# Sums by destination over a span of 64 nodes instead of 128 in a graph network kernel

## The chip, the cores and the metric

The kernel runs on one core of a Trainium2 chip. The metric is the time of one execution on the device, in microseconds (us), as the median of several runs. The engines are TensorE (PE, with its weight loads listed as PEld), VectorE (DVE), ScalarE (ACT), GpSimd (POOL) and SyncE (SP). SP issues most of the plain transfers, POOL the indirect ones.

## The reference, cut to what matters

There are 6250 nodes with 128 features and 206250 directed edges, sorted by their destination `dst`. Each node is also an edge to itself in that list. Two layers follow one another:

```python
edge_index = jnp.stack([src, dst])
h = jnp.maximum(_layernorm(x), 0.0)
# layer 0: row = src, col = dst, self loops added, deg = segment_sum(w, row)
#   w_norm = dinv[row] * w * dinv[col];  out = segment_sum(w_norm * (h @ kernel)[col], row)
x = x + relu(out + bias)
h = jnp.maximum(_layernorm(x), 0.0)
# layer 1: heads = src, tails = dst
#   msg_fwd  = concat(h[src], edge_attr) @ W_fwd  + b_fwd   -> summed at dst
#   msg_back = concat(h[dst], edge_attr) @ W_back + b_back  -> summed at src
#   divided by the number of messages, leaky relu, + h, layer norm with gamma and beta
x = x + layer1(...)
```

By linearity the kernel sums raw rows first and multiplies by the weights at the end. It so needs, among others, the sum of `edge_attr` rows by `src` and the sum of `edge_attr` rows by `dst`. The second of these is what the change is about, along with one step of layer 0.

## The kernel before, in words

The edges are cut into 202 groups of 1024 (`GE`), each as 128 partitions by 8 chunks (`J`). Since edges are sorted by `dst`, a group touches a short run of consecutive destinations. 206250 / 6250 is 33 edges for each node, so 1024 edges cover about 31 nodes. The first destination of a group is its base (`base_i`), and `rel` is `dst` minus the base. `setup_and_degrees` computes both, and sets a flag when any `rel` is above 127 or below 0; then a general path without spans is taken (`nc.Else`), else the path described here. The span ("window") of a group is the 128 nodes from its base on.

`first_layer` treats groups 0 to 107 (`G1` = 108) together with half of layer 0. `dense_sums` treats the other 94 (`NB`) together with dense products over 25 double tiles of nodes: six groups ahead of the first tile, then four with each of 22 tiles. The last three tiles have no groups beside them. Both hold the same pieces for each group, in an order written out by hand for each engine:

- SP loads `rel` of the group broadcast to all partitions (`rel_b`, first layer only), the source keys in the same way (`key_b`), the records (`rec`), the 128 rows of `g` from the base on (`window`, first layer only) and the 1024 edge attributes (`attrs`).
- DVE's `prepare`, one step a chunk, compares keys (`same`) and in the first layer, at chunk 2, builds `spread_hot` (L857): partition n, column e is 1 where edge e has `rel` = n. DVE's `spot_sums` (L828, L1690) builds `sum_hot`: for each edge on a partition and each of 8 chunks, a one-hot of its `rel`. It waits until TensorE is through with the group before.
- TensorE's `spread` (L952, first layer only) multiplies `spread_hot` by `window`, so that each edge gets the row of `g` of its destination. `sum_chunk` (L965, L1815) multiplies the chunk's attributes, as the loaded weights, with `sum_hot` as the moving operand; 8 of them add up in one PSUM bank, `win_bank`. At chunk 2 it first waits for `window_added` and `sum_ready`, and then makes the products of chunks 0, 1 and 2 at once. Each float32 product is two weight loads and two matmuls in the trace. L969, L970 and L1817 multiply by `same`, for the sums by source.
- DVE's `add_window` (L837, L1699) adds `win_bank` to `attr_sums` at the base. It stands right behind `spot_sums` in DVE's order, and both stand at chunk 0 of a group.
- ACT copies the sums by source out of PSUM (L1042, L1898), and POOL adds them to tables in DRAM with one indirect DMA for each chunk (L814, L1646), in four tables in turn.

Around them in `dense_sums`: DVE's `one_hots` (L1742, L1746, L1747) and the additions L1782; TensorE's L1797 (pair counts), L1853 and L1873 (products of counts and features), L1838 (transposes). In the first layer: DVE's L885, L886, L891 and L900, and TensorE's L1001, L979 and L991.

Of the kernel before, what the change touches and what calls it, by code (L numbers as in the profile page):

```python
# [29 lines left out]
BF16 = mybir.dt.bfloat16  # L30
I16 = mybir.dt.int16
I32 = mybir.dt.int32
ALU = mybir.AluOpType
# [5 lines left out]
F = 128  # L39
P = 128  # L40
NP, NT = 125, 50
J = 8
# [27 lines left out]
GPI = 4  # L70
G1 = GPI * (2 * DS + 1)
# [32 lines left out]
def setup_and_degrees(nc, d):  # L104
# [4 lines left out]
    with ExitStack() as ctx:  # L109
# [236 lines left out]
        def _(dve):  # L346
# [94 lines left out]
            def offsets():  # L441
# [9 lines left out]
                nc.vector.tensor_scalar(wide[:, 0:1], wide[:, 0:1], P - 0.5, None, ALU.is_gt)  # L451
# [228 lines left out]
def first_layer(nc, d):  # L680
# [10 lines left out]
    with ExitStack() as ctx:  # L691
# [14 lines left out]
        rel_b = sb("rel_b", [P, 2, P, J], BF16)  # L706
        window = sb("window", [P, 2, F])
        attrs = sb("attrs", [P, 2, J, F])
        spread_hot = sb("spread_hot", [P, J, P])
        same = sb("same", [P, J, P])  # L710
        sum_hot = sb("sum_hot", [P, J, P])
# [62 lines left out]
        def _(sp):  # L774
            everywhere = lambda a, g: a[group_at(g)].rearrange("(o e) -> o e", o=1).to_broadcast([P, GE])
            flat = lambda t: t.rearrange("p q j -> p (q j)")

            def slot(i, kk, last):
                k = 2 * i + kk
                for gi in range(GPI):  # L780
# [3 lines left out]
                    sp.dma_start(flat(rel_b[:, h, :, :]), everywhere(d.dst_offset, g)).then_inc(rel_in[h], 16)  # L784
                    sp.dma_start(flat(key_b[:, h, :, :]), everywhere(d.src_key, g)).then_inc(key_in[h], 16)
# [6 lines left out]
                    sp.dma_start(window[:, h, :], d.g[bass.ds(base, P), :]).then_inc(window_in[h], 16)  # L792
# [31 lines left out]
        def _(dve):  # L824
            def spot_sums(g, h):

                at_least(dve, summed, J * g)
                nc.vector.tensor_tensor(sum_hot[:], iota_c.unsqueeze(1).to_broadcast([P, J, P]), rec[:, h, 2, :].unsqueeze(2).to_broadcast([P, J, P]),  # L828
                                        ALU.is_equal).then_inc(sum_ready, 1)

            def add_window(g):
# [4 lines left out]
                at = bass.ds(base, P)  # L836
                nc.vector.tensor_tensor(d.attr_sums[:, at], d.attr_sums[:, at], win_bank[:, 0:P], ALU.add).then_inc(window_added, 1)  # L837

            def prepare(i, kk, gi, j, ahead):
# [103 lines left out]
        def _(pe):  # L943
# [11 lines left out]
            def sum_chunk(i, kk, gi, j):  # L955
# [8 lines left out]
                for jj in (range(3) if j == 2 else range(j, j + 1) if j > 2 else ()):  # L964
                    nc.tensor.matmul(win_bank[:, 0:P], attrs[:, h, jj, :], sum_hot[:, jj, :], start=(jj == 0), stop=(jj == J - 1))  # L965
# [490 lines left out]
def dense_sums(nc, d):  # L1456
# [10 lines left out]
    with ExitStack() as ctx:  # L1467
# [38 lines left out]
        sum_hot = shared(J * P).rearrange("p (j q) -> p j q", j=J)  # L1506
# [159 lines left out]
        def _(dve):  # L1666
# [20 lines left out]
            def spot_sums(q, p):  # L1687

                at_least(dve, chunk_done, J * q)
                nc.vector.tensor_tensor(sum_hot, d.iota[:].unsqueeze(1).to_broadcast([P, J, P]), rec[:, p, 2, :].unsqueeze(2).to_broadcast([P, J, P]),  # L1690
                                        ALU.is_equal).then_inc(sum_ready, 1)

            def add_window(q):
# [4 lines left out]
                here = bass.ds(base, P)  # L1698
# [615 lines left out]
```

## Time and profile before

| | us |
|---|---|
| median of 3 runs | 4362.68 (4362.0 to 4367.89) |
| profiled execution, its own time | 4383.92 |
| span of the profiled execution | 4382.1 |
| setup | 0 to 478 |
| first layer, 108 groups | 478 to 2206 |
| end of layer 0, node by node | 2206 to 2413 |
| dense sums, six groups ahead | 2413 to 2500 |
| dense sums, 22 tiles with four groups each | 2500 to 4066 |
| dense sums, last tiles | 4066 to 4188 |
| last nodes | 4188 to 4382 |

The profile gives for each engine the time it was busy, and for each instruction the idle time ahead of it and what ended that. "Granted clock" is the share of TensorE's full clock of 2.4 GHz that it had; 0.50 is 1.2 GHz. The stages' bounds are read from the first and last indirect DMA of each stage and the first instructions of the next.

### The profile page before, as it was taken

How to read it: one execution, taken by the hardware profiler on the slowest of the kernel's cores; microseconds unless marked ns; L12 is line 12 of the kernel's file. 1: busy time of each engine (PE TensorE's matmuls, PEld its weight loads, DVE VectorE, ACT ScalarE, POOL GpSimd, SP SyncE). 2: the span in 40 equal slices, each digit the busy share in tenths (PEclk: the TensorE clock that was granted, in tenths of full speed). 3: DMA queues.
4: the chain of work that ended last, by engine and by line, in shares of the span. 5: the costliest groups of instructions: out<-in, count | busy, mean ns of one | idle time of the engine just before them, and what ended most of it. 6: DMA issues, size and time to landing. Idle time of an engine off the chain costs nothing. (4 is left out here: it accounts for less than half of the span.)

```text
span 4382.1 us, 100155 instructions
## 1 busy us (share of the span) xinstructions
PE 3372.6 (77%) x30313; PEld 2825.5 (64%) x30529; DVE 3169.7 (72%) x8053; ACT 1866.7 (43%) x4498; POOL 3001.3 (68%) x1812
## 2 busy tenths in 40 slices
PE   1444599888888988889712599888988898889945
PEld 1344587777777877777612577676767676777635
DVE  6999898888888888888524777666666666666427
ACT  1030355555555555555404244444444444444513
POOL 2665588888888888888810788777777777788210
PEclk9989899999999999999956699999999999999977
DMA  9990678777777777877785555445444544454861
GB/s 162 290 212 14 134 143 143 138 139 142 138 139 143 135 139 142 142 138 143 116 148 122 89 85 83 76 78 82 77 76 77 79 77 78 76 83 72 97 124 30
DMA packets 682053, 504.17 MB, mean 115 GB/s; under 512 B 308854, under 2 KB 593920, under 8 KB 679754
## 3 DMA queue, kind: packets, MB, share of 16 engines
q0 software_dynamic: 260032, 176.60, 36.2%
q1 hardware_dynamic: 421475, 320.75, 29.6%
q8 instruction: 287, 4.70, 0.4%
q14 instruction: 259, 2.12, 0.2%
HBM read 283.43 MB, written 240.12 MB: 119 GB/s over the span
## 5 line engine op out<-in xcount | busy, mean ns | idle before, releaser
L1646 POOL DMA_INDIRECT gcn_sums<-shared,ds_to_i x752 | 1290.0, 1715 | 569.8 <-ACT shared L1898 353.6
L814 POOL DMA_INDIRECT gcn_sums<-fl_sums,fl_to_i x864 | 1439.0, 1665 | 290.0 <-DMA gcn_sums<-fl_sums,fl_to_i 149.1
L1853 PE MATMUL bank<-ds_counts,ds_parts 128*128 128x256 bf16 x3675 | 605.9, 278 | 0.0
L1922 ACT COPY ds_turned<-bank 128x1024 bf16<-128x1024 bf16 (+1 forms) x325 | 313.1, 963 | 619.0 <-PE bank L1838 619.0
L1042 ACT COPY fl_sums<-bank 128x256 f32<-128x256 f32 x864 | 324.8, 376 | 575.4 <-PE bank L970 504.5
L1886 ACT CAST ds_counts<-bank 128x392 bf16<-128x392 f32 x800 | 382.2, 490 | 228.9 <-PE bank L1797 216.2
L852 DVE SCALAR_TENSOR_TENSOR fl_same<-fl_key_b,fl_pat,bank 128x128 f32<-128x128 bf16 x864 | 371.6, 442 | 102.7 <-PE bank L970 85.7
L1873 PE MATMUL bank<-ds_turned,ds_now 128*128 128x512 bf16 (+1 forms) x1734 | 434.3, 382 | 11.3
L1782 DVE TENSOR_TENSOR src_sums<-src_sums,bank 128x512 f32<-128x512 f32 (+1 forms) x325 | 213.2, 656 | 292.4 <-PE bank L1873 287.8
L1815 PE MATMUL bank<-shared 128*128 128x128 f32 x1504 | 304.3, 306 | 119.3 <-DVE attr_sums L1699 91.3
L1712 DVE SCALAR_TENSOR_TENSOR shared<-shared,ds_pat,from_me 128x128 f32<-128x128 bf16 x752 | 312.7, 443 | 103.9 <-PE bank L1817 92.4
L965 PEld LDWEIGHTS bank<-fl_sum_hot,fl_attrs 128*128 128x128 f32 x1728 | 263.8, 192 | 184.3 <-issue 112.2
L969 PE MATMUL bank<-fl_pay,fl_same 128*128 128x128 f32 x1728 | 349.3, 285 | 41.6 <-issue 31.4
L1817 PE MATMUL bank<-shared 128*128 128x128 f32 x1504 | 318.4, 295 | 75.3 <-DVE shared L1712 52.3
L965 PE MATMUL bank<-fl_sum_hot,fl_attrs 128*128 128x128 f32 x1728 | 324.4, 290 | 57.5 <-DVE attr_sums L837 57.3
L1853 PEld LDWEIGHTS bank<-ds_counts,ds_parts 128*128 128x128 bf16 x3675 | 344.8, 100 | 32.2
L1001 PE MATMUL bank<-fl_hi_w,fl_lo_hot 128*128 128x98 bf16 x4992 | 288.9, 208 | 83.7 <-DVE fl_hi_w L891 83.7
L970 PE MATMUL bank<-fl_attrs,fl_same 128*128 128x128 f32 x1728 | 340.9, 280 | 0.0
L991 PE MATMUL bank<-fl_turned,fl_g_tile 128*128 128x512 f32 (+1 forms) x676 | 333.3, 575 | 3.7 <-DVE gcn_t L900 1.6
L969 PEld LDWEIGHTS bank<-fl_pay,fl_same 128*128 128x128 f32 x1728 | 273.9, 196 | 82.9 <-issue 71.0
L1001 PEld LDWEIGHTS bank<-fl_hi_w,fl_lo_hot 128*128 128x128 bf16 x4992 | 257.1, 98 | 106.8 <-issue 87.5
L891 DVE TENSOR_TENSOR fl_hi_w<-fl_hi_hot,fl_twos 128x784 bf16<-128x784 bf16 x624 | 317.2, 564 | 8.7
(256 smaller groups left out, 7004.1 us busy)
## 6 DMA issues: line engine op xcount, KB each, us to landing
fl_attrs<-in_edge_attr SPq DMA_DIRECT2D x108, 512.0 KB
shared<-in_edge_attr SPq DMA_DIRECT2D x186, 256.0 KB
fl_rel_b<-dst_offset SPq DMA_DIRECT2D x108, 256.0 KB
fl_key_b<-src_key SPq DMA_DIRECT2D x108, 256.0 KB
gcn_sums<-zeros SPq DMA_DIRECT2D x40, 640.0 KB
shared<-src_key SPq DMA_DIRECT2D x94, 256.0 KB
gcn_sums<-fl_sums,fl_to_i POOLq DMA_INDIRECT x864
near<-src_float SPq DMA_DIRECT2D x1, 12892.0 KB
```

Source lines behind the costliest of these rows:

```text
L814: nc.gpsimd.indirect_dma_start(out=d.tab_gcn[j % K], out_offset=bass.IndirectOffsetOnAxis(ap=to_i[:, (GPI * kk + gi) % 4, j:j + 1], axis=0 ...
L852: nc.vector.scalar_tensor_tensor(same[:, j, :], key_p[:, h, :, j], pat_f[:, j:j + 1], from_me_c, ALU.is_equal, ALU.mult, accum_out=later[: ...
L965: nc.tensor.matmul(win_bank[:, 0:P], attrs[:, h, jj, :], sum_hot[:, jj, :], start=(jj == 0), stop=(jj == J - 1))
L969: nc.tensor.matmul(sum_bank[j % 2][:, 0:F], same[:, j, :], pay[:, j // U, j % U, :], start=True, stop=True)
L970: nc.tensor.matmul(sum_bank[j % 2][:, F:2 * F], same[:, j, :], attrs[:, h, j, :], start=True, stop=True).then_inc(summed, 1)
L991: nc.tensor.matmul(prod_bank[:, 0:n], g_tile[:, old, :], turned[:, (old + b) % 2, 0:n], start=True, stop=True).then_inc(prod_ready, 1)
L1001: last = nc.tensor.matmul(pair_bank[:, c * HH:(c + 1) * HH], lo_hot[:, go % 2, q, :], hi_w[:, go % 2, m, q, :], start=(m == 0), stop=(m == 2))
L1042: nc.scalar.copy(sums[:, h, j, :], sum_bank[j % 2][:, 0:2 * F]).then_inc(staged, 1)
L1646: nc.gpsimd.indirect_dma_start(out=d.tab_gcn[j % K].rearrange("n (two f) -> (n two) f", two=2), out_offset=bass.IndirectOffsetOnAxis(ap=to ...
L1853: ins = nc.tensor.matmul(row_bank[:, 0:2 * P], parts[:, tile, s, :], counts[:, h, tile, :, :].rearrange("p b q -> p (b q)"), start=(tile = ...
L1873: ins = nc.tensor.matmul(back_bank[v][:, 0:n], now[:, h, half, s, :], turned[:, v, half, 0:n], start=(half == 0 and s == 0), stop=(half == ...
L1886: nc.scalar.copy(to, pair_bank[batch % B][:, 0:PB * HH].rearrange("p (c k) -> p k c", c=PB)).then_inc(pair_copied, 1)
```

## The change

A constant `W` = 64 takes the place of 128 as the width of the span. In both passes `sum_hot` is built for 64 columns instead of 128, the products with it have 64 moving columns, and `add_window` adds 64. In the first layer `rel_b`, `window` and `spread_hot` have 64 partitions: the two transfers are half as large, the compare L857 runs on half the partitions with the same number of columns, and the product `spread` sums over 64 rows. The flag for the general path is set from `rel` above 63. The number of instructions, of transfers and of waits, and their order, stay.

```diff
+W = 64
...
-                nc.vector.tensor_scalar(wide[:, 0:1], wide[:, 0:1], P - 0.5, None, ALU.is_gt)
+                nc.vector.tensor_scalar(wide[:, 0:1], wide[:, 0:1], W - 0.5, None, ALU.is_gt)
...
-        rel_b = sb("rel_b", [P, 2, P, J], BF16)
-        window = sb("window", [P, 2, F])
+        rel_b = sb("rel_b", [W, 2, P, J], BF16)
+        window = sb("window", [W, 2, F])
...
-        spread_hot = sb("spread_hot", [P, J, P])
+        spread_hot = sb("spread_hot", [W, J, P])
...
-        sum_hot = sb("sum_hot", [P, J, P])
+        sum_hot = sb("sum_hot", [P, J, W])
...
-                    sp.dma_start(flat(rel_b[:, h, :, :]), everywhere(d.dst_offset, g)).then_inc(rel_in[h], 16)
+                    sp.dma_start(flat(rel_b[:, h, :, :]), everywhere(d.dst_offset, g, W)).then_inc(rel_in[h], 16)
...
-                    sp.dma_start(window[:, h, :], d.g[bass.ds(base, P), :]).then_inc(window_in[h], 16)
+                    sp.dma_start(window[:, h, :], d.g[bass.ds(base, W), :]).then_inc(window_in[h], 16)
...
-                nc.vector.tensor_tensor(sum_hot[:], iota_c.unsqueeze(1).to_broadcast([P, J, P]), rec[:, h, 2, :].unsqueeze(2).to_broadcast([P, J, P]),
+                nc.vector.tensor_tensor(sum_hot[:], iota_c[:, 0:W].unsqueeze(1).to_broadcast([P, J, W]), rec[:, h, 2, :].unsqueeze(2).to_broadcast([P, J, W]),
...
-                nc.vector.tensor_tensor(d.attr_sums[:, at], d.attr_sums[:, at], win_bank[:, 0:P], ALU.add).then_inc(window_added, 1)
+                nc.vector.tensor_tensor(d.attr_sums[:, at], d.attr_sums[:, at], win_bank[:, 0:W], ALU.add).then_inc(window_added, 1)
...
-                    nc.vector.tensor_scalar(spread_hot[:], rel_b[:, h, :, :].rearrange("p q j -> p j q"), d.part[:, 0:1], None,
+                    nc.vector.tensor_scalar(spread_hot[:], rel_b[:, h, :, :].rearrange("p q j -> p j q"), d.part[0:W, 0:1], None,
...
-                    nc.tensor.matmul(win_bank[:, 0:P], attrs[:, h, jj, :], sum_hot[:, jj, :], start=(jj == 0), stop=(jj == J - 1))
+                    nc.tensor.matmul(win_bank[:, 0:W], attrs[:, h, jj, :], sum_hot[:, jj, :], start=(jj == 0), stop=(jj == J - 1))
```

In `dense_sums` the lines of `spot_sums`, `add_window` and `sum_chunk` change in the same way; there the constant that `spot_sums` reads is `d.iota` in SBUF, where the first layer's is in PSUM.

## Rows read from the trace of the kernel before

**Rows 1.** Stretches: us, busy PE, PEld, DVE, ACT, POOL; granted clock, DMA share, GB/s.
```profile
478.00:2206.00 1728.00, 1507.98 (x13854) 1308.34 (x13854) 1415.58 (x4017) 919.57 (x2482) 1438.98 (x864) 0.97 0.78 138
...
2413.00:2500.00 87.00, 42.42 (x270) 38.27 (x270) 66.93 (x155) 18.16 (x37) 67.25 (x35) 0.63 0.47 83
2500.00:4066.00 1566.00, 1392.60 (x12677) 1113.00 (x12877) 1044.54 (x2717) 705.78 (x1227) 1222.73 (x718) 0.96 0.49 78
```

**Rows 2.** Instruction groups, POOL, first layer: busy us, mean ns, idle before, releasers.
```profile
L814 POOL DMA_INDIRECT gcn_sums<-fl_sums,fl_to_i x864 | 1439.0, 1665 | 290.0 <-DMA gcn_sums<-fl_sums,fl_to_i 149.1 <-issue 115.3 <-ACT fl_sums L1042 24.9
```

**Rows 3.** Timeline of POOL, first layer: start, us, and idle time before in brackets.
```profile
1204.78 1.56 POOL L814 DMA_INDIRECT gcn_sums<-fl_sums,fl_to_i  x1 [0.30 <-issue]
1206.65 2.41 POOL L814 DMA_INDIRECT gcn_sums<-fl_sums,fl_to_i  x1 [0.30 <-ACT fl_sums L1042]
```

**Rows 4.** Instruction groups, POOL, 2500 to 4066 us.
```profile
L1646 POOL DMA_INDIRECT gcn_sums<-shared,ds_to_i x718 | 1223.3, 1704 | 343.0 <-issue 192.5 <-ACT shared L1898 138.0 <-DMA gcn_sums<-shared,ds_to_i 12.5
```

**Rows 5.** Who TensorE waited for, 2500 to 4066 us: total us, times, longest.
```profile
PE bank L1815 <- DVE attr_sums L1699: 58.9, 37, 2.6
```

**Rows 6.** Timeline of PE and DVE around one wait of a dense tile.
```profile
3047.43 0.69 DVE L1782 TENSOR_TENSOR src_sums<-src_sums,bank 128x512 f32<-128x512 f32 x1 [0.89 <-PE bank L1873]
...
3048.03 0.49 DVE L1742 COPY ds_twos<-places 128x256 bf16 x2
...
3048.56 1.23 DVE L1746 TENSOR_TENSOR ds_lo_hot<-ds_numbers,ds_twos 128x2048 bf16<-128x2048 bf16 x1
...
3049.18 0.49 PE L1853 MATMUL bank<-ds_counts,ds_parts 128*128 128x256 bf16 x3
3049.70 0.97 DVE L1747 TENSOR_TENSOR ds_hi_hot<-ds_numbers,ds_twos 128x1568 bf16<-128x1568 bf16 x1
...
3050.59 1.22 DVE L1690 TENSOR_TENSOR shared<-iota,ds_rec 128x1024 f32<-128x1024 f32 x1
3051.72 0.28 DVE L1699 TENSOR_TENSOR attr_sums<-attr_sums,bank 128x128 f32 x1
...
3052.06 0.93 PE L1815 MATMUL bank<-shared 128*128 128x128 f32 x6 [2.39 <-DVE attr_sums L1699]
```

**Rows 7.** 1.7 to 3.1 us behind such waits, two of 22: us, busy PE, clock, DMA.
```profile
2565.95:2567.35 1.40, 1.40 (x5) 0.50 0.53 47
2633.31:2634.71 1.40, 1.40 (x11) 1.00 0.55 47
```

**Rows 8.** The stretch behind the wait of Rows 6, columns as in Rows 1.
```profile
3053.40:3056.80 3.40, 3.40 (x14) 1.62 (x12) 0.85 (x3) 0.37 (x1) 2.27 (x2) 0.50 0.30 24
```

**Rows 9.** As Rows 7, behind first-layer waits of 1.8 to 2.0 us, two of 19.
```profile
713.94:715.34 1.40, 1.40 (x20) 1.00 0.82 100
...
1099.09:1100.49 1.40, 1.40 (x8) 0.50 0.78 97
```

**Rows 10.** Timeline of PE and its weight loads at one product of the span.
```profile
3002.88 0.34 PE L1797 MATMUL bank<-ds_hi_hot,ds_lo_hot 128*128 128x98 bf16 x4
...
3003.01 0.19 PEld L1815 LDWEIGHTS bank<-shared 128*128 128x128 f32 x1
...
3003.06 0.45 PE L1815 MATMUL bank<-shared 128*128 128x128 f32 x2
...
3003.12 0.19 PEld L1815 LDWEIGHTS bank<-shared 128*128 128x128 f32 x1
...
3003.34 0.39 PE L1817 MATMUL bank<-shared 128*128 128x128 f32 x2
```

**Rows 11.** Instruction groups of the first layer that lose partitions or rows.
```profile
L952 PE MATMUL bank<-fl_window,fl_spread_hot 128*128 128x128 f32 x1728 | 234.2, 280 | 19.9 <-DVE fl_spread_hot L857 19.9
...
L857 DVE TENSOR_SCALAR fl_spread_hot<-fl_rel_b,part 128x1024 f32<-128x1024 bf16 x108 | 126.8, 1174 | 0.0
```

**Rows 12.** Transfers of the page that the change halves, out<-in, count, size of one.
```profile
fl_rel_b<-dst_offset SPq DMA_DIRECT2D x108, 256.0 KB
```

More of the change, by code:

```diff
@@ L774, in _ @@
         def _(sp):
-            everywhere = lambda a, g: a[group_at(g)].rearrange("(o e) -> o e", o=1).to_broadcast([P, GE])
+            everywhere = lambda a, g, n: a[group_at(g)].rearrange("(o e) -> o e", o=1).to_broadcast([n, GE])
             flat = lambda t: t.rearrange("p q j -> p (q j)")
@@ L783, in slot @@
                     sp.sem_inc(load_turns, 1)
-                    sp.dma_start(flat(rel_b[:, h, :, :]), everywhere(d.dst_offset, g)).then_inc(rel_in[h], 16)
-                    sp.dma_start(flat(key_b[:, h, :, :]), everywhere(d.src_key, g)).then_inc(key_in[h], 16)
+                    sp.dma_start(flat(rel_b[:, h, :, :]), everywhere(d.dst_offset, g, W)).then_inc(rel_in[h], 16)
+                    sp.dma_start(flat(key_b[:, h, :, :]), everywhere(d.src_key, g, P)).then_inc(key_in[h], 16)
                     at_least(sp, sum_ready, g - 1)
@@ L835, in add_window @@
                 at_least(dve, window_added, g)
-                at = bass.ds(base, P)
-                nc.vector.tensor_tensor(d.attr_sums[:, at], d.attr_sums[:, at], win_bank[:, 0:P], ALU.add).then_inc(window_added, 1)
+                at = bass.ds(base, W)
+                nc.vector.tensor_tensor(d.attr_sums[:, at], d.attr_sums[:, at], win_bank[:, 0:W], ALU.add).then_inc(window_added, 1)
             def prepare(i, kk, gi, j, ahead):
@@ L1505, in dense_sums @@
         same = shared(J * P).rearrange("p (j q) -> p j q", j=J)
-        sum_hot = shared(J * P).rearrange("p (j q) -> p j q", j=J)
+        sum_hot = shared(J * W).rearrange("p (j q) -> p j q", j=J)
         sums = shared(4 * U * F).rearrange("p (u j f) -> p u j f", u=4, j=U)
@@ L1689, in spot_sums @@
                 at_least(dve, chunk_done, J * q)
-                nc.vector.tensor_tensor(sum_hot, d.iota[:].unsqueeze(1).to_broadcast([P, J, P]), rec[:, p, 2, :].unsqueeze(2).to_broadcast([P, J, P]),
+                nc.vector.tensor_tensor(sum_hot, d.iota[:, 0:W].unsqueeze(1).to_broadcast([P, J, W]), rec[:, p, 2, :].unsqueeze(2).to_broadcast([P, J, W]),
                                         ALU.is_equal).then_inc(sum_ready, 1)
@@ L1697, in add_window @@
                 at_least(dve, window_added, q)
-                here = bass.ds(base, P)
-                nc.vector.tensor_tensor(d.attr_sums[:, here], d.attr_sums[:, here], win_bank[:, 0:P], ALU.add).then_inc(window_added, 1)
+                here = bass.ds(base, W)
+                nc.vector.tensor_tensor(d.attr_sums[:, here], d.attr_sums[:, here], win_bank[:, 0:W], ALU.add).then_inc(window_added, 1)
             def prepare(i, h, gi, j, ahead):
@@ L1814, in sum_chunk @@
                 for jj in (range(3) if j == 2 else range(j, j + 1) if j > 2 else ()):
-                    nc.tensor.matmul(win_bank[:, 0:P], attrs[:, jj // U, jj % U, :], sum_hot[:, jj, :], start=(jj == 0), stop=(jj == J - 1))
+                    nc.tensor.matmul(win_bank[:, 0:W], attrs[:, jj // U, jj % U, :], sum_hot[:, jj, :], start=(jj == 0), stop=(jj == J - 1))
                 pe.wait_ge(same_ready, ch + 1)
```

## The prediction

> **What bounds the kernel now.** I read the stretches first. The two passes over the edges take 1728 and 87 + 1566 us of the 4382.1 us span, and the change touches nothing outside them but one constant in a compare. In the first layer PE, DVE and POOL are all busy for more than 80% of the time [rows 1], so shares don't say which one sets the pace. The groups of instructions do: POOL's 864 indirect issues are busy for 1439.0 us and are preceded by 290.0 us of idle time [rows 2], together 1729 us, the whole stretch. The timeline shows why that idle time is no slack: an issue takes at least 1.56 us and 0.30 us pass before each, whoever is named as the releaser [rows 3]. 864 x 1.86 = 1607 us is the floor. The other 122 us are 91 us by which issues run longer than 1.56 us, as the one of 2.41 us does, and 31 us of idle time above 0.30 us. The first layer is bound by POOL's issues, and these are as many after the change.
>
> In the dense pass it is otherwise. There 718 issues take 1223.3 us, and with 0.30 us for each 1439 us of 1566 [rows 4], so POOL has some 127 us to spare, 5.8 us a tile. PE is busy for 1393 of the 1566 us [rows 1] and goes from product to product. The table of waits says what stops it: 37 times, for 58.9 us, it waits for `add_window` (L1699) [rows 5]. One such wait stands in each of the 22 tiles and has 2.4 to 2.6 us; the other 15 are of 0.2 us. The timeline shows its making: PE has nothing left behind L1853 at 3049.2, while DVE goes through L1782, L1742, L1746 and L1747 and only then through `spot_sums` (L1690, 1.22 us) and `add_window` (L1699, 0.28 us); PE starts 0.06 us behind its end, after 2.39 us idle [rows 6]. So two instructions that the change makes shorter stand at the end of the chain that PE waits for.
>
> That wait costs more than itself. Behind 19 of the 22, PE works at a granted clock of 0.50, which is 1.2 GHz; behind the other three at 2.4 GHz [rows 7]. The low stretch is 3.4 us long, full of work [rows 8], so it costs about 1.7 us.
>
> **The change part by part.** *The one-hots and the addition.* L1690 has 1024 columns and starts 1.13 us ahead of L1699; L1699 has 128 columns and 0.28 us [rows 6]. From the two durations, (1.22 - 0.28) / 896 is 1.05 ns a column. Taking 512 columns off the one and 64 off the other saves 0.54 + 0.06 = 0.60 us a group. The bounds are nothing, if an instruction has a floor at this size, and half of both, 0.75 us. In the 22 long waits this is on the path: 13 us. The 15 short ones disappear: 3 us. In the other groups of the tiles DVE has done both before PE asks, and the gain is idle time of DVE.
>
> *The clock behind the waits.* The waits shrink to 1.8 to 2.0 us. The dense pass has hardly any of that length, but the first layer has 19 waits of 1.8 to 2.0 us, and behind 5 of them the clock is low, behind 14 not [rows 9]. By that share 6 of 22 would be followed by a low stretch, if nothing changes 19. I take 10, between them and nearer the measured share of like waits: 9 x 1.7 = 15 us. The bounds are 0 and 13 x 1.7 = 22 us.
>
> *The six groups ahead of the tiles.* DVE is busy for 67 of 87 us there while PE and POOL have gaps [rows 1], and DVE carries five pairs of the two instructions: 5 x 0.60 = 3 us, between 0 and 4.
>
> *The narrower product.* Halving the moving columns of L1815 and L965 could halve their time, but I cost it at nothing, because the weight load sets the pace. A float32 load of L1815 begins at 3003.01, as the last 98-column matmul of L1797 enters, and the second load begins at 3003.12: 0.11 us for one load, with little in the array to hide it. The product's two matmuls take 0.28 us from start to start of the next product instead of L1817's 0.23 us, since the first waits for its load [rows 10]. A load takes as long as 128 columns of matmul do now, so 64 columns leave the array waiting for the next load. The Trainium skill, "TensorE: Matmul & The Clock Gate", LDWEIGHTS, states that a load takes its columns divided by 1.2, 107 ns here, whatever the number of rows, and the section on weight-path modes that the fast load is not for float32. By that rule the saving is nothing too, and the trace agrees with its 0.11 us.
>
> *64 partitions in the first layer.* L857 keeps its 1024 columns and so its 1.17 us; L952 keeps 128 columns in load and matmul [rows 11]. Neither is on the path, since POOL covers both. If that cover were gone, `spot_sums` and `add_window` would give 108 x 0.60 = 65 us there. As POOL holds the pace they give nothing. The transfers `rel_b` shrink from 256 to 128 KB a group [rows 12], `window` by half too, while the DMA engines are at 0.78 [rows 1]. What can come of it is part of POOL's 31 us of idle time above 0.30 us, where it waits for earlier scatters to land. I take 3 us, between 0 and 31. The 91 us of longer issues I leave as they are.
>
> *The flag.* 64 nodes hold 64 x 33 = 2112 edges on average, twice a group, so no group reaches `rel` = 64 and the general path isn't taken.
>
> The sum: 13 + 3 + 15 + 3 + 3 = 37 us, 4383.9 to 4347 us in the profiled execution. That one is 21 us above the median of the runs, so against the median: 4362.7 - 37 = 4326 us. With all low bounds it is 13 us off (4350), with all high ones 13 + 3 + 22 + 4 + 31 = 73 us (4290).
>
> **Rivals.** *The gain is given back.* PE comes 0.6 us earlier to its next product in each tile and waits there for ACT, or the clock stays low behind the shorter wait as before and the phase of the tile shifts instead. Then only the groups ahead and a few transfers count: about 4357 us. For it speaks that DVE and ACT wait often on PE in a ring; against it, that L1699 is the largest wait of PE in the tiles [rows 5].
>
> *The columns set the pace.* Then L1815 saves 0.055 us in each of 16 matmuls a group: 88 groups x 16 x 0.055 = 77 us, 3.5 us a tile, which with the rest still fits in POOL's spare 5.8 us: 4326 - 77 = 4249 us. The first layer would not follow, as POOL holds it. Against it speak [rows 10]. The Trainium skill's same page, Back-to-back issue gap, gives for a matmul alone a time that follows its columns, which is this rival's rule; it counts no loads.
>
> *Slower: the product over 64 rows loses its cover.* L952 alone uses half of the array's rows. If the change between 64 and 128 rows kept its loads from running beside matmuls, each of its 16 matmuls a group would take 0.11 us longer [rows 10], 1.8 us a group and 190 us in all. PE is idle for 220 us of the first layer [rows 1], but much of that is needed where it waits for DVE. With half of it as cover, the first layer gets 80 us longer: 4326 + 80 = 4406 us. It decides from about 1 us a group on. No row of the kernel before has a product over 64 rows, so only the instruction's unchanged columns speak against it.
>
> **How the numbers follow.** The forecast has 0.68, the gain given back 0.17, the columns 0.08 and the slower case 0.07. The forecast's own range is 4290 to 4350 us. To leave out no more than 2 in 10, the range goes from 4290 to 4362 us: it takes in the case given back and leaves out the two others, with 0.15. A measurement of this kernel tells about 0.2%, 9 us, from no change. The forecast is beyond it save for its last edge, and so are the columns: faster 0.75. The case given back falls within it: same 0.18. Slower 0.07.
>
> **What would show it.** In the profile after: first layer again 1720 to 1730 us with 0.30 us before most issues of POOL; L1690 and L828 at 0.65 to 0.7 us and L1699 at about 0.22 us; one wait of L1815 a tile, of 1.8 to 2.0 us; low clock behind fewer than 15 of these; L1815's pairs still 0.22 to 0.28 us from start to start; L952 at 280 ns. The prediction is wrong if the first layer moves by more than 15 us either way, or if PE's wait moves to another line and the tiles keep their 71 us.

## The result and the profile after

The change makes the kernel slower. It takes 4416.57 us (median of 4 runs, 4412.54 to 4421.14), and the kernel before takes 4365.28 us on the same chip (4 runs, 4362.0 to 4371.42). The ratio is 1.0111, with a 95% interval of 1.0091 to 1.013, so 51 us are lost where 37 were forecast to be gained. The profiled execution took 4412.54 us, its span is 4410.7 us.

The stretches of the kernel after, cut at the same places and with the columns of [rows 1]:

```profile
478.00:2276.00 1798.00, 1610.68 (x13854) 1363.35 (x13854) 1355.42 (x4023) 895.90 (x2482) 1523.15 (x865) 0.94 0.74 124
2486.00:2574.00 88.00, 50.13 (x272) 45.08 (x272) 66.92 (x168) 18.23 (x37) 68.79 (x38) 0.54 0.50 81
2574.00:4094.00 1520.00, 1364.45 (x12647) 1101.07 (x12844) 998.67 (x2701) 703.99 (x1222) 1189.43 (x714) 0.97 0.52 80
```

The first layer grows from 1728 to 1798 us, and the 22 tiles shrink from 1566 to 1520 us. DVE is less busy in both, so the shorter instructions are there. In the first layer TensorE's and POOL's busy times rise, from 1508 to 1611 us and from 1439 to 1523 us. The groups of instructions say which of its terms grew (busy us, mean ns, idle before):

```profile
L815 POOL DMA_INDIRECT gcn_sums<-fl_sums,fl_to_i x864 | 1522.8, 1762 | 274.9 <-issue 129.2 <-DMA gcn_sums<-fl_sums,fl_to_i 127.6 <-ACT fl_sums L1043 18.0
...
L966 PE MATMUL bank<-fl_sum_hot,fl_attrs 128*128 128x64 f32 x1728 | 298.4, 277 | 0.4
...
L953 PE MATMUL bank<-fl_window,fl_spread_hot 64*128 64x128 f32 x1728 | 261.9, 294 | 19.9 <-DVE fl_spread_hot L858 19.9
...
L858 DVE TENSOR_SCALAR fl_spread_hot<-fl_rel_b,part 64x1024 f32<-64x1024 bf16 x108 | 124.0, 1149 | 0.0
L829 DVE TENSOR_TENSOR fl_sum_hot<-bank,fl_rec 128x512 f32<-128x512 f32 x108 | 73.9, 685 | 39.1 <-issue 23.7 <-PE bank L971 13.4 <-DVE fl_to_i L866 0.5
```

The 864 issues of [rows 2] still pass without slack, but one takes 1762 ns in the mean instead of 1665. 1522.8 less 864 x 1.56 is 175 us of longer issues, where it was 91. POOL's idle time above 0.30 us fell from 31 to 16 us, so nothing waits more for its data. The first layer is longer by the length of its own issues (84 us more) and loses nothing elsewhere. L829 has 0.685 us for 512 columns where L828 had 1.22 us for 1024, as forecast.

The timeline shows the new long issue. POOL's and DVE's rows overlap in time (start, us, idle before in brackets):

```profile
1562.44 2.27 POOL L815 DMA_INDIRECT gcn_sums<-fl_sums,fl_to_i  x1 [0.30 <-issue]
1565.02 3.16 POOL L815 DMA_INDIRECT gcn_sums<-fl_sums,fl_to_i  x1 [0.30 <-issue]
1568.48 1.56 POOL L815 DMA_INDIRECT gcn_sums<-fl_sums,fl_to_i  x1 [0.30 <-issue]
...
1562.11 1.16 DVE L858 TENSOR_SCALAR fl_spread_hot<-fl_rel_b,part 64x1024 f32<-64x1024 bf16 x1
...
1565.22 1.52 DVE L892 TENSOR_TENSOR fl_hi_w<-fl_hi_hot,fl_twos 128x784 bf16<-128x784 bf16 x3
```

The issue at 1562.44 begins while the compare L858 runs, and ends at 1564.71, which is 1.44 us behind the compare's end at 1563.27. I call such an issue held. Held issues stood in the kernel before too: the one of 2.41 us in [rows 3] ends at 1209.06, 1.44 us behind a one-hot of DVE (L886). They could even be held by several DVE instructions in a row, if they began beside the first of them. In the kernel before an issue begins 0.35 us into the three multiplies `hi_w`, which follow one another without a gap (a train), and ends 1.44 us behind the last:

```profile
918.33 2.63 POOL L814 DMA_INDIRECT gcn_sums<-fl_sums,fl_to_i  x1 [0.30 <-issue]
...
917.98 1.54 DVE L891 TENSOR_TENSOR fl_hi_w<-fl_hi_hot,fl_twos 128x784 bf16<-128x784 bf16 x3
```

New in the kernel after is the issue at 1565.02: it begins 0.20 us ahead of such a train. It ends at 1568.18, 1.44 us behind the end of the whole train (1566.74). 29 issues of this first layer take over 3.1 us; in the kernel before none takes over 2.64.

The train is not the only place. Sorted by the DVE instruction that ends 1.44 us ahead of an issue's end, the 84 us come from three kinds: behind the compare 33 issues are held to the end of a `hi_w` train (what they take beyond 1.56 us sums to 49 us; before the change 6 issues and 4 us) and 20 to the end of the one-hot `lo_hot` (21 us, before 4 issues and 3 us), and 22 that begin beside the compare are held past its end, to that of `hi_hot` or `gcn_t` (25 us). The compare itself holds 46 issues, where it held 56, which takes 4 us off.

In the 22 tiles TensorE's waits for DVE, to be compared with [rows 5], and two stretches behind such waits, to be compared with [rows 7]:

```profile
PE bank L1816 <- DVE attr_sums L1700: 43.1, 22, 2.0
...
2765.11:2766.51 1.40, 1.40 (x12) 0.85 (x10) 0.19 (x1) 0.17 (x1) 1.17 (x1) 1.00 0.56 47
2830.96:2832.36 1.40, 1.40 (x5) 0.54 (x4) 0.00 (x0) 0.00 (x0) 1.17 (x1) 0.50 0.55 47
```

There are 22 waits of 1.75 to 2.03 us where there were 22 of 2.35 to 2.63; the 15 short ones are gone. Behind 7 of the 22 the granted clock is low, as in the second stretch (0.50, which is 1.2 GHz); it was low behind 19 of 22.

### The profile page after: what moved, and what is told of

It is laid out like the page before. It is cut to its first block and busy times, and to the rows that moved or that the text cites. A ratio compares the mean times of both kernels' runs of the same rounds, so it can differ in the third digit from the quotient of the medians.

```text
span 4410.7 us, 100155 instructions
## 1 busy us (share of the span) xinstructions
PE 3456.7 (78%) x30313; PEld 2876.8 (65%) x30529; DVE 3063.1 (69%) x8053; ACT 1843.7 (42%) x4498; POOL 3056.4 (69%) x1812
## 5 line engine op out<-in xcount | busy, mean ns | idle before, releaser
L815 POOL DMA_INDIRECT gcn_sums<-fl_sums,fl_to_i x864 | 1522.8, 1762 | 274.9 <-issue 129.2
L1647 POOL DMA_INDIRECT gcn_sums<-shared,ds_to_i x752 | 1261.4, 1677 | 557.8 <-ACT shared L1899 343.1
L970 PE MATMUL bank<-fl_pay,fl_same 128*128 128x128 f32 x1728 | 392.9, 310 | 75.3 <-ACT fl_sums L1043 38.3
L1874 PE MATMUL bank<-ds_turned,ds_now 128*128 128x512 bf16 (+1 forms) x1734 | 418.9, 371 | 11.7 <-issue 0.4
L1818 PE MATMUL bank<-shared 128*128 128x128 f32 x1504 | 352.5, 318 | 72.4 <-DVE shared L1713 48.6
L966 PEld LDWEIGHTS bank<-fl_sum_hot,fl_attrs 128*128 128x128 f32 x1728 | 273.6, 199 | 123.6 <-issue 114.2
L1816 PE MATMUL bank<-shared 128*128 128x64 f32 x1504 | 274.6, 287 | 98.4 <-DVE attr_sums L1700 71.1
L892 DVE TENSOR_TENSOR fl_hi_w<-fl_hi_hot,fl_twos 128x784 bf16<-128x784 bf16 x624 | 315.5, 558 | 8.7
L586 PE MATMUL bank<-col_w,row_hot 128*128 128x200 bf16 x1616 | 164.9, 258 | 196.0 <-DVE col_w L508 196.0
```

Source lines behind the costliest of these rows:

```text
L815: nc.gpsimd.indirect_dma_start(out=d.tab_gcn[j % K], out_offset=bass.IndirectOffsetOnAxis(ap=to_i[:, (GPI * kk + gi) % 4, j:j + 1], axis=0 ...
L970: nc.tensor.matmul(sum_bank[j % 2][:, 0:F], same[:, j, :], pay[:, j // U, j % U, :], start=True, stop=True)
L1647: nc.gpsimd.indirect_dma_start(out=d.tab_gcn[j % K].rearrange("n (two f) -> (n two) f", two=2), out_offset=bass.IndirectOffsetOnAxis(ap=to ...
L1818: nc.tensor.matmul(sum_bank[:, j % U * F:(j % U + 1) * F], same[:, j, :], attrs[:, half, j % U, :], start=True, stop=True).then_inc(chunk_ ...
L1874: ins = nc.tensor.matmul(back_bank[v][:, 0:n], now[:, h, half, s, :], turned[:, v, half, 0:n], start=(half == 0 and s == 0), stop=(half == ...
```

## The experiments

In the code of the experiments the constant `W` is split in three, so that parts of the change can be taken alone: `WS` for what belongs to `spread` (the transfers `rel_b` and `window`, the compare, the product's rows), `WH` for the first layer's `spot_sums`, its products and `add_window`, and `WD` for the same in the dense pass. 64 everywhere is the whole change, 128 everywhere the kernel before (but for the flag's threshold, which stays at 64).

Each time below is the median of its runs and stands beside runs of the kernel before on the same chip. The ratio is the one on record, which is not quite the quotient of the two medians. "First layer" is from its first issue to the end of its last, "long issues" is what its 864 issues take over 1.56 us, summed. The last two columns are counted in the rows of POOL and DVE. "Held" are issues over 2.56 us that start within 2.5 us behind the end of a spread compare. The last column takes those issues that start 0.18 to 0.22 us ahead of a `hi_w` train that follows within eight DVE instructions of the compare, and says how many of them took over 2.3 us.

| kernel | us | ratio [95%] | first layer | long issues | held | at 0.2 us |
|---|---|---|---|---|---|---|
| before | 4365 to 4373 | 1 | 1721 | 91 | 3 | 0 of 24 |
| after | 4416.6 | 1.0111 [1.0091, 1.013] | 1790 | 175 | 48 | 28 of 33 |
| e1 `WH` only | 4374.7 | 1.001 [0.9992, 1.0027] | 1717 | 89 | 0 | 0 of 26 |
| e2 `WS` only | 4416.6 | 1.0099 [1.0071, 1.0126] | 1759 | 122 | 46 | 9 of 14 |
| e3 `WD` only | 4351.5 | 0.9948 [0.9923, 0.9973] | 1714 | 86 | 4 | 0 of 31 |
| e4 `WH` = 96 only | 4371.5 | 1.0008 [0.9992, 1.0023] | 1723 | 86 | 2 | 0 of 20 |
| g1 product 128 rows | 4415.8 | 1.0088 [1.0072, 1.0105] | 1788 | 173 | 53 | 27 of 41 |
| g2 product 64, rest of spread 128 | 4347.4 | 0.9931 [0.9914, 0.9948] | 1723 | 94 | 2 | 0 of 32 |
| g3 spread all 128 | 4342.6 | 0.9923 [0.9903, 0.9944] | 1722 | 94 | 3 | 0 of 26 |
| g4 g3 + repeated products | 4336.5 | 0.9906 [0.9888, 0.9924] | 1731 | 102 | 3 | 0 of 31 |
| h1 g2 + `rel_b` 64 | 4347.6 | 0.9953 [0.9935, 0.997] | 1712 | 95 | 3 | 0 of 30 |
| h2 g2 + compare 64 | 4442.6 | 1.0187 [1.0154, 1.022] | 1811 | 182 | 55 | 28 of 31 |
| h3 g2 + `window` 64 | 4358.8 | 0.9973 [0.9941, 1.0004] | 1721 | 90 | 2 | 0 of 21 |
| h4 after, keys first | 4442.6 | 1.0184 [1.0153, 1.0214] | 1806 | 187 | 54 | 30 of 33 |
| i1 after, compare 128 | 4334.4 | 0.9916 [0.9899, 0.9934] | 1711 | 94 | 2 | 0 of 19 |
| i2 g2 + compare 96 | 4441.2 | 1.0166 [1.0149, 1.0183] | 1815 | 185 | 53 | 31 of 36 |
| i3 h2 + small operation | 4451.0 | 1.0182 [1.0151, 1.0213] | 1828 | 200 | 50 | 0 of 1 |
| j1 h2 + wait | 4335.8 | 0.9913 [0.9896, 0.993] | 1712 | 82 | 0 | none |
| j2 h2 + second half | 4439.4 | 1.0149 [1.0132, 1.0166] | 1807 | 154 | 24 | 21 of 21 |
| k1 after + wait | 4330.1 | 0.9906 [0.9878, 0.9934] | 1690 | 72 | 0 | 0 of 1 |

**Which part.** The first four kernels only set constants:

```diff
# e1_hot_only          # e2_spread_only       # e3_dense_only        # e4_hot96
+WS = 128              +WS = 64               +WS = 128              +WS = 128
+WH = 64               +WH = 128              +WH = 128              +WH = 96
+WD = 128              +WD = 128              +WD = 64               +WD = 128
```

> Only the one-hots of the first layer, their product and their addition have 64 columns; the spread part of the first layer and the whole dense pass stay at 128. Theory A (DVE, freed of 0.6 us a group, runs up to POOL's pace and then stands at fixed places of POOL's issues, which it holds up): the first layer takes about 70 us longer, as after the whole change, 4435 us in all, with issues of about 1.76 us on average. Theory B (the 64 partitions of the spread part, in compare, product or transfers, hold up the issues): the first layer stays at 1721 us from its first to its last issue, 4365 us in all.

> Only the spread part of the first layer (rel_b, window, spread_hot, the product over 64 rows) is halved; the one-hots of both passes stay at 128 columns. Theory A: no change, 4360 to 4370 us, issues of 1.67 us on average. Theory B: 70 us longer, about 4435 us, issues of about 1.76 us.

> The first layer is as before; only the dense pass has 64 columns. Both theories: the first layer stays at 1721 us, the dense pass gains the 41 us that it gained after the whole change, 4325 us in all. If the dense gain hung on the first layer in some way, it would be less than 30 us.

> As the first of these runs, but with 96 columns in place of 64 in the one-hots of the first layer: 0.3 us a group come off DVE instead of 0.6 us. Theory A: issues longer than before, by an amount that depends on where DVE then stands and needn't lie between those of 128 and 64 columns; between 4365 and 4450 us, and not equal to the kernel before if ACT waits for scatters to land for over 150 us. Theory B: 4365 us.

Theory A, that a DVE with less work in the first layer runs up to POOL's pace and holds its issues, falls with e1 and e4, which change nothing. Of the three parts only the spread part loses time: 47 us alone. That this is nearly the 51 us of the whole change is chance. e2's first layer is 38 us longer than the kernel before's, the whole change's 69 us, and the whole change gets some back in the dense pass. With 128 columns in `sum_hot` the issues meet the trains at other places (14 at 0.2 us in e2, 33 after the whole change), so the size of the loss hangs on the other parts too. The dense part alone gains 18 us, where both theories had 41. In the profiles the dense pass, from its first to its last issue, takes 1637 to 1638 us in e1, e2 and e4 and 1619 us in e3. The 1652 us of the kernel before's profile were thus 14 us more than its own code gives in three other profiles.

**The product or what feeds it.** `spread` has three parts at 64: the transfers, the compare and the product's rows.

```diff
# g1_product128: the whole change, tiles of 128 partitions, the upper 64 rows zero
-        window = sb("window", [WS, 2, F])
-        spread_hot = sb("spread_hot", [WS, J, P])
+        window = sb("window", [P, 2, F])
+        spread_hot = sb("spread_hot", [P, J, P])
# g2_product64: WS = 128, and
-   ..., spread_hot[:, half * U + q, :], window[:, h, :], start=True, stop=True)
+   ..., spread_hot[0:64, half * U + q, :], window[0:64, h, :], start=True, stop=True)
# g3_no_spread: WS = 128, WH = WD = 64
# g4_repeats: g3, and in spread
-                for q in range(U):
+                for q in (0, 0, 1, 2, 3, 3):
```

> The whole change, but the product of the spread part sums over 128 rows again, the upper 64 of spread_hot and window being zeroed once; the transfers and the compare keep their 64 partitions. Theory P (TensorE's loads for 64 rows don't run beside matmuls of 128 rows, so that each spread block begins and ends with 0.2 us of wait, and this costs the first layer its time): first layer 1715 to 1725 us from first to last issue, about 4350 us in all. Theory T (transfers into 64 partitions, or a compare over 64, hold up POOL's issues): first layer 1790 us, 4416 us in all, as the changed kernel.

> The whole change, but the transfers and the compare of the spread part are at 128 partitions again, and only its product sums over 64 rows. Theory P: as the changed kernel, first layer about 1790 us, 4416 us in all. Theory T: first layer about 1720 us, 4350 us in all.

> The whole change but for the spread part of the first layer, which is at 128 partitions throughout. Both theories: first layer 1715 to 1725 us, dense pass as with the dense part alone; the first two single parts add up to the kernel before less 18, about 4350 us.

> As the run without the spread part, but each spread block makes its first and its last product twice, at 128 rows: two more float32 products of 0.22 us at the places where the 64-row product has its waits, 0.9 us a group. If TensorE's lost time as such is what costs the first layer, it gets as long as with 64 rows, 1760 to 1790 us, 4400 us in all or more. If it takes a pause of the array (through the granted clock, which falls behind idle stretches), it stays below 1740 us, 4365 us in all.

The product over 64 rows costs nothing (g2), and undoing it brings nothing back (g1). TensorE's busy time in g2's first layer is 1588 us, most of the rise seen after the change, and the layer is as long as before (1723 us). g4 adds four products to each group. Its first layer is 9 us longer than g3's (1731 against 1722 us), which is far from the 66 us that g1 has over g3; its median is no higher, as its dense pass, the same code, happened to be 14 us shorter in the profile. So TensorE's lost time costs a few us at most. What is left is the transfers and the compare.

**Transfer, compare or window.** Each is cut to 64 alone, on top of g2:

```diff
# h1_rel64 (rel_b[64:128] is set to 0 once, so the compare gives zeros there)
+   sp.dma_start(flat(rel_b[0:64, h, :, :]), everywhere(d.dst_offset, g, 64))
# h2_compare64
+   nc.vector.tensor_scalar(spread_hot[0:64, :, :], rel_b[0:64, h, :, :]..., d.part[0:64, 0:1], None, ALU.is_equal)
# h3_window64
+   sp.dma_start(window[0:64, h, :], d.g[bass.ds(base, 64), :])
# h4_key_first: the whole change, with the transfer of key_b ahead of that of rel_b
```

> The kernel that keeps the product over 64 rows but transfers and compares on 128 partitions (4347 us, first layer 1723 us) with one thing changed back: the offsets' transfer writes 64 partitions (128 KB instead of 256 KB a group); the compare still covers 128 partitions, the upper 64 rows of the offsets hold a constant. Theory R (the narrower transfer of offsets is the cause: it moves the loads behind it on the queue, and with them what collides with POOL's issues): about 4400 to 4416 us, first layer 1760 to 1790 us, long issues over 0.15 s-e-3, that is over 150 us in sum. Theory C (the compare on 64 partitions) and theory V (the window's load of 64 rows): 4340 to 4355 us, first layer 1715 to 1730 us, long issues 90 to 100 us in sum.

> The same kernel with both transfers into 128 partitions and only the compare that makes the spread one-hots cut to 64 partitions. Theory C: 4400 to 4416 us, long issues of the first layer 150 us or more in sum. Theories R and V: 4340 to 4355 us, long issues 90 to 100 us. If no one of the three parts gives more than 15 us by itself, the loss needs two of them together, and none of these theories stands.

> The same kernel with only the window's load cut to 64 rows (32 KB instead of 64 KB a group), offsets and compare on 128 partitions. Theory V: 4400 to 4416 us. Theories R and C: 4340 to 4355 us. I take V for the least likely, since the load is small and PE's wait for it does not show in the trace.

> The whole change, with the keys' transfer (256 KB, 128 partitions) issued ahead of the offsets' (128 KB, 64 partitions) instead of behind it. If the loss comes from when the transfers of a group land beside POOL's issues, this order moves the time: by more than 15 us off 4416, most likely down, with the long issues of the first layer at another sum than 174 us. If it comes from the compare, or from 64 partitions as such wherever they lie in time, the time stays within 8 us of 4416 and the sum of long issues at 165 to 185 us.

The compare on 64 partitions is the cause: 4442.6 us, against 4347.4 us in g2 and 4347.6 us in h1, which ran on h2's chip. The narrower transfers do not lengthen the first layer. h3's 11 us over g2 are not told apart from no change: its first layer and dense pass are as long as g2's (1721 and 1613 us against 1723 and 1616), and its first layer starts 12 us later than g2's, behind a setup that the edit does not touch. h4 went the other way from its expectation's "most likely down", 26 us up; with the compare as the cause, the order of the transfers shifts where issues and trains meet, and I have no run that says more.

The two kernels g2 and h2 differ in this one compare. Here is the same place in each, first g2, with the compare on 128 partitions:

```profile
1446.59 2.28 POOL L818 DMA_INDIRECT gcn_sums<-fl_sums,fl_to_i  x1 [0.30 <-issue]
1449.17 1.56 POOL L818 DMA_INDIRECT gcn_sums<-fl_sums,fl_to_i  x1 [0.30 <-DMA gcn_sums<-fl_sums,fl_to_i]
...
1446.26 1.15 DVE L861 TENSOR_SCALAR fl_spread_hot<-fl_rel_b,part 128x1024 f32<-128x1024 bf16 x1
...
1449.37 1.53 DVE L895 TENSOR_TENSOR fl_hi_w<-fl_hi_hot,fl_twos 128x784 bf16<-128x784 bf16 x3
```

and h2, with the compare on 64:

```profile
1507.27 2.28 POOL L818 DMA_INDIRECT gcn_sums<-fl_sums,fl_to_i  x1 [0.30 <-issue]
1509.86 3.16 POOL L818 DMA_INDIRECT gcn_sums<-fl_sums,fl_to_i  x1 [0.30 <-issue]
...
1506.94 1.17 DVE L861 TENSOR_SCALAR fl_spread_hot<-fl_rel_b,part 64x1024 f32<-64x1024 bf16 x1
...
1510.04 1.54 DVE L895 TENSOR_TENSOR fl_hi_w<-fl_hi_hot,fl_twos 128x784 bf16<-128x784 bf16 x3
```

Both compares hold the issue beside them for 2.28 us. The next issue starts 0.20 and 0.18 us ahead of the same train. In g2 it passes in 1.56 us, in h2 it is held to the train's end. The last column of the table makes this general. Where the compare covers 128 partitions, 0 of 260 such issues are held, in ten kernels. Where it covers 64 or 96, it is 174 of 210, in eight without a wait. The distance in time is the same, so the places where the engines meet do not explain the difference. They still decide which issues are caught: in the same eight kernels only 2 of 115 are held that begin 0.23 to 0.30 us ahead of the train. A second place shows the same contrast. Of the issues that begin 0.3 to 0.4 us behind the compare's end, ahead of the one-hots, 9 of 390 take over 2.3 us in the ten kernels with 128 partitions, and 80 of 173 in after, e2, g1, h2, h4 and i2.

**What of the compare does it.**

```diff
# i1_compare128: the whole change, the compare over 128 partitions as in h1
# i2_compare96: as h2, [0:96]
# i3_small_op: h2, and behind the compare
+   nc.vector.tensor_scalar(small[:, h, :], numbers[:, 0:8], d.part[:, 0:1], None, ALU.is_equal)
# j1_wait_behind: h2, and behind the compare
+   dve.wait_ge(spread_ready, g + 1)
# j2_two_halves: h2, and ahead of the compare
+   nc.vector.tensor_scalar(spread_hot[64:128, :, :], rel_b[64:128, h, :, :]..., d.part[64:128, 0:1], None, ALU.is_equal)
# k1_change_wait: the whole change with j1's line
```

> The whole change, with the spread compare alone kept on 128 partitions (the upper 64 rows of the offsets hold a constant; transfers, window and product use 64). Theory C (the compare on 64 partitions is the whole loss): 4335 to 4360 us, first layer 1710 to 1725 us, long issues about 95 us in sum. A rival, that 64-row transfers cost together what they did not cost one by one: over 4375 us.

> The kernel of the compare on 64 partitions alone (4443 us), the compare on 96 partitions. If each operation of fewer than 128 partitions leaves the wake: 4430 to 4450 us, long issues about 180 us in sum, over 50 issues held over 1 us within 2.5 us behind the compare. If it is the number 64 or the lower half: 4340 to 4360 us, long issues about 94 us, under 5 such issues.

> The kernel of the compare on 64 partitions alone (4443 us), with a compare of 8 elements on 128 partitions right behind it on VectorE, its result unused. If the wake is a state that the last operation of that form leaves behind, the small operation ends it: 4345 to 4375 us, long issues about 95 to 110 us. If the wake comes from what the other engines do in that time (PE reading 64 rows, a transfer), it stays: 4430 to 4450 us, long issues about 180 us.

> The kernel of the compare on 64 partitions alone (4443 us), with VectorE waiting for the compare's own completion ahead of its next operation. If the hold of the second issue belongs to a train of operations that runs on without a gap from the compare: back to 4350 to 4375 us, long issues of the first layer about 95 us in sum. If it doesn't: 4435 to 4455 us, long issues about 180 us, over 50 issues held over 1 us behind the compare.

> The same kernel with a second compare, of the other 64 partitions, ahead of the first (nothing reads it). VectorE has 108 times 1.1 us more, 119 us. If any operation on part of the partitions leaves the hold behind: issues held over 1 us longer behind the compare stay over 50, and the time is 4460 to 4520 us. If what counts is that all 128 partitions are written before the next issue: under 10 such issues behind the second compare, and the time 4380 to 4440 us.

> The whole change, with VectorE waiting for the end of its spread compare (64 partitions) ahead of its next operation. If the hold behind that compare is the whole loss: 4330 to 4350 us, first layer 1710 to 1725 us, long issues 80 to 95 us in sum, under 5 issues held over 1 us within 2.5 us behind the compare. If something else of the change costs time: over 4375 us.

96 partitions do the same as 64 (i2). A second compare for the other half does not help (j2: 21 of 21 are held at 0.2 us, though for 2.7 us and not 3.16; the 24 held in all are fewer, and its 4439 us came in under my lower bound of 4460. Its first layer is 84 us longer than g2's, of which 60 us are longer issues and the rest is idle time of POOL, beside a DVE that is busy for 138 us more). A small operation on 128 partitions behind the compare doesn't either (i3): it moves the train 0.13 us away from the issue, to 0.32 to 0.36 us, and 32 of 40 are held there. One wait for the compare's own end takes the loss away (j1, k1): no issue is held, and the long issues sum to 82 and 72 us. j1's 4335.8 us is under the 4350 to 4375 us that I expected, and k1's first layer of 1690 us under its 1710 us: in k1 also fewer issues are held by the compare itself (16 instead of 56 in the kernel before), as they meet it elsewhere. A place in k1, with the wait as the 0.21 us ahead of L905; the issue of 2.29 us begins a microsecond ahead of the compare there and is not held by it:

```profile
1462.83 2.29 POOL L818 DMA_INDIRECT gcn_sums<-fl_sums,fl_to_i  x1 [0.30 <-issue]
1465.43 1.57 POOL L818 DMA_INDIRECT gcn_sums<-fl_sums,fl_to_i  x1 [0.31 <-DMA gcn_sums<-fl_sums,fl_to_i]
1467.30 1.56 POOL L818 DMA_INDIRECT gcn_sums<-fl_sums,fl_to_i  x1 [0.30 <-DMA gcn_sums<-fl_sums,fl_to_i]
...
1463.88 1.16 DVE L861 TENSOR_SCALAR fl_spread_hot<-fl_rel_b,part 64x1024 f32<-64x1024 bf16 x1
1465.25 0.69 DVE L905 TENSOR_TENSOR gcn_t<-gcn_t,bank 128x512 f32<-128x512 f32 x1 [0.21 <-DVE fl_spread_hot L861]
```

And one in k1 where the compare does hold an issue (553.30, for 1.97 us). The next begins 1.76 us behind the compare's end, as the one at 1565.02 in the kernel after does (1.75 us), and passes in 1.56 us:

```profile
553.30 1.97 POOL L818 DMA_INDIRECT gcn_sums<-fl_sums,fl_to_i  x1 [0.30 <-issue]
555.58 1.56 POOL L818 DMA_INDIRECT gcn_sums<-fl_sums,fl_to_i  x1 [0.30 <-DMA gcn_sums<-fl_sums,fl_to_i]
...
552.67 1.15 DVE L861 TENSOR_SCALAR fl_spread_hot<-fl_rel_b,part 64x1024 f32<-64x1024 bf16 x1
553.85 0.69 DVE L905 TENSOR_TENSOR gcn_t<-gcn_t,bank 128x512 f32<-128x512 f32 x1
...
555.90 1.51 DVE L896 TENSOR_TENSOR fl_hi_w<-fl_hi_hot,fl_twos 128x784 bf16<-128x784 bf16 x3
```

In j1 and k1 together 46 issues begin 1.7 to 1.8 us behind the compare's end, and none takes over 2.3 us; in h2 31 of 37 do.

The groups of the issues in k1:

```profile
L818 POOL DMA_INDIRECT gcn_sums<-fl_sums,fl_to_i x864 | 1420.3, 1644 | 278.0 <-issue 122.3 <-DMA gcn_sums<-fl_sums,fl_to_i 118.8 <-ACT fl_sums L1047 34.7
```

and in i1:

```profile
L818 POOL DMA_INDIRECT gcn_sums<-fl_sums,fl_to_i x864 | 1441.7, 1669 | 278.3 <-DMA gcn_sums<-fl_sums,fl_to_i 144.8 <-issue 107.6 <-ACT fl_sums L1047 23.5
```

k1, the whole change and one wait, has the lowest median of this study: 4330.13 us (4326.4 to 4335.06) against 4372.38 us of before. i1's 4334.44 us (4328.76 to 4339.18) is not told apart from it.

## Why the prediction was wrong

**The step that failed** is the one on 64 partitions in the first layer. It costed the compare L857 at nothing because its columns and its own time stay, and closed with "The 91 us of longer issues I leave as they are". The compare's own time did stay (1174 to 1149 ns). But an issue behind it is now held by the next train of DVE, and the 91 us became 175. This one term was +84 us, and it was taken as zero, with no bound of its own. The first layer moved by 69 us, past the 15 us that the prediction had named as its sign of being wrong. [rows 2] and [rows 3] held the hint: I read from them that POOL sets the pace, and left unread what makes some of its issues 2.4 us long. Laid beside DVE's rows, 165 of the 189 issues over 1.7 us end 1.44 us behind a DVE instruction. The effect of the partitions could not be seen there, since the kernel before has no compare on fewer than 128.

**The rest of the sum came out near, in part by luck.** i1 has all of the change but the compare on fewer partitions, and gains 35 us against 37 forecast. k1 gains 42 us, but that is no test of the sum: its first layer is 31 us shorter than the kernel before's, which the forecast had at 3. The bounds were also added up wrongly: the low sum keeps the 13 us of the one-hots, though their own lower bound was nothing.

- One-hots and addition: 16 us forecast for long and short waits of the tiles; 58.9 - 43.1 = 15.8 us measured between the two profiles. e1, e2 and e4, with the old code of the dense pass, have only 1 to 3 short waits and 53.3 to 53.9 us in all, so about 10 us are the change's: 0.45 us a long wait, where I had 0.60.
- Clock behind the waits: I forecast 10 low stretches of 22; there are 7, and 7, 8 and 9 in g2, i1 and k1. But e1, e2 and e4, with the dense pass of before, have 13, 14 and 15 where the profile of before has 19. So the term is the difference from 13 to 19 down to about 8, 9 to 19 us at 1.7 us each, beside the 15 forecast.
- Six groups ahead: 3 us forecast. From the first issue of the dense pass to its 41st it takes 93.9 us after, and 96.8 to 97.5 us in before, e1, e2 and e4.
- The whole dense pass: 1611 to 1617 us in twelve of the sixteen kernels with the change there (1597, 1619, 1621 and 1625 us in g4, e3, i3 and j2), against 1637 to 1638 us in the three experiments with its old code, so 20 to 27 us of the 34 that I had; the kernel before's profile, from which I counted, was itself 14 us long there.
- Smaller transfers: 3 us forecast. h1's first layer is 11 us shorter than g2's, but starts 9 us later, and its median is the same (4347.6 and 4347.4 us). i1's is as short as h1's (1711 us) without a later start, but first layers whose spread part is untouched go from 1714 us (e3) to 1723 us. The 3 us are neither shown nor excluded.
- The narrower product: it gives nothing, as forecast, though its own time does follow its columns. From the start of a pair of L1816 to the start of the next product pass 0.233 us, with L1815 it was 0.287 us (medians, 564 cases without a wait). But from the start of a pair of L1818, which stands behind it and keeps its 128 columns, to what follows it pass 0.277 us, where it was 0.224 us (691 cases). The two together take 0.51 us before and after. The groups say the same, first before, then after:

```profile
L1817 PE MATMUL bank<-shared 128*128 128x128 f32 x1418 | 294.3, 290 | 20.6 <-ACT shared L1898 17.8 <-issue 2.9
L1815 PE MATMUL bank<-shared 128*128 128x128 f32 x1418 | 278.7, 299 | 81.8 <-DVE attr_sums L1699 58.9 <-ACT shared L1898 23.0
...
L1818 PE MATMUL bank<-shared 128*128 128x128 f32 x1410 | 319.3, 309 | 20.6 <-ACT shared L1899 17.8 <-issue 2.8
...
L1816 PE MATMUL bank<-shared 128*128 128x64 f32 x1408 | 246.7, 277 | 65.3 <-DVE attr_sums L1700 43.1 <-ACT shared L1899 22.2
```

L1816 is busy for 32 us less than L1815, and L1818 for 25 us more than L1817.

**The rivals.** The slower one gave 4406 us, near the measured 4416, by another mechanism. Its mechanism is partly real. Behind a block of products over 64 rows the next weight load starts 0.200 us after the start of the block's last matmul (median of 216 blocks in the kernels after and g2), and 0.002 us after it in g1, where the products have 128 rows. Twice a group that is 43 us of TensorE in the first layer, not the 190 us that the rival supposed, and g2 shows that the cover holds: it costs nothing. That the columns set the pace came true in neither pass: what the narrower product saves, the one behind it takes. The gain was not given back in the tiles either: TensorE's waits shrank, and the clock was low behind 7 of them.

**The trace and the skill.** The traces show issues of POOL that have begun when a long DVE instruction runs and finish 1.44 us behind its end, and, behind a compare on fewer than 128 partitions, 1.44 us behind the last of three multiplies. The Trainium skill, "SBUF — State Buffer", Who interferes with whom, says that DVE and GpSimd share one pair of ports as an exclusive lock, which one of them has for one whole instruction, and that an operation with two SBUF inputs takes only its read side, so that writing descriptors would not wait for it (it calls that inferred). The first half agrees with the issues of 2.28 us. The inference does not fit this case: the multiplies L892 have two SBUF inputs, and they hold the issue at 1565.02 for all three of their instructions, as L891 holds the one at 918.33 in the kernel before. No run here tells whether it is the writing of descriptors that waits or the reading of `fl_to_i`, and the page does have such an operation contend with a GpSimd instruction that reads SBUF.

**What stays open.** Why a compare on fewer partitions does this, and why a wait ends it. The wait puts DVE's next instruction mostly 0.21 us behind the compare's end (0.03 us in the second place shown from k1) instead of 0.08 us ahead of it, so it breaks the run of overlapping instructions. It also moves where issues and trains meet: in k1 47 issues start within 0.02 us of the train's start and only one 0.2 us ahead of it. i3's shift of 0.13 us alone did not end the hold, which speaks for the break. A few issues of j1 and k1 allow a closer comparison: four begin 1.75 to 1.77 us behind the compare's end and 0.32 to 0.34 us ahead of the train, as in i3, the one at 555.58 among them. None of the four is held, where 32 of i3's 40 are. That speaks for the break too, but four cases don't prove it.

## What to carry to other kernels

When an engine's queue sets the pace, look at how long its instructions are and what the other engines run beside the long ones, not only at its waits: POOL had less idle time after than before, and was slower. Where VectorE works beside indirect transfers of POOL, an operation on fewer partitions can cost time though its columns stay; try it at 128 partitions, and with a wait for its end behind it. Of a change with several parts, run those costed at nothing by themselves: here one line stood between a loss of 51 us and a gain of 42.

## What was not expected of the hardware

- An indirect issue of POOL that begins beside a DVE compare of 1024 columns ends 1.44 us behind it (2.27 to 2.28 us instead of 1.56 in three of the cases shown). Behind a compare on 64 or 96 partitions the following issue, if it begins 0.2 us ahead of three multiplies, is mostly held through them, 3.16 us (174 of 210); behind one on 128 partitions never (0 of 260).
- The first weight load behind products over 64 rows starts 0.200 us after the last of their matmuls has started, that behind products over 128 rows 0.002 us after.
- A float32 product with 64 moving columns instead of 128 was 0.054 us shorter, and the product of 128 columns behind it 0.053 us longer.
- The same code of the dense pass had a low granted clock behind 13, 14, 15 and 19 of 22 waits of 2.4 us in four profiles.
